# V made token-major for two head pairs in one product, in two half pairs of four

## The reference

```
xn  = layernorm(x)
K, Q, V = xn @ W_K[h], xn @ W_Q[h], xn @ W_V[h]        # per head h: 1024 x 64
attn = softmax(causal(Q K^T) / 8);  z = attn @ V;  a = concat(z) @ W_O^T
m = sum over the top 2 of 9 experts of w * (silu(xn Wg[e]) * (xn Wu[e])) @ Wd[e]
out = x + a + m
```

## Time and profile before

| | |
|---|---|
| median of 3 runs | 722.73 us |
| the profiled execution | 724.33 us, its span 722.4 us |
| granted TensorE clock, mean | 0.983 |
| busy: TensorE, VectorE, ScalarE, GpSimd | 97%, 87%, 78%, 67% |
| chain that ended last: TensorE, VectorE, DMA, GpSimd | 86%, 4%, 3%, 3% |
| one half of attention | 35.3 to 35.6 us |

### The profile page before, as it was taken

How to read it: one execution, slowest core, us unless ns; L and a number is a source line. 1 busy time by engine, 2 the same in 40 slices (tenths; PEclk the granted TensorE clock), 3 DMA queues, 4 the chain that set the end, 5 groups by cost and what they waited for, 6 DMA issues and landing times.

```text
span 722.4 us, 15068 instructions
## 1 busy us (share of the span) xinstructions
PE 698.1 (97%) x4877; PEld 607.4 (84%) x4877; DVE 629.8 (87%) x1401; ACT 564.5 (78%) x1312; POOL 487.2 (67%) x494
## 2 busy tenths in 40 slices
PE   7879999899999999999999999999999999999997
PEld 6659999778888888888888888888888888888886
DVE  8967777768999999999999999999999998998986
ACT  5915555568888888888888888888888888888873
POOL 5464444157677777878686878787878786868761
PEclk9869999989999999999999999999999999999999
DMA  8514722132434242424242424242515151515001
GB/s 237 165 30 111 168 75 58 44 90 69 92 74 105 54 103 63 107 52 107 59 107 52 106 62 111 49 116 50 125 34 130 36 135 24 136 27 139 19 2 59
DMA packets 50236, 61.05 MB, mean 85 GB/s; under 512 B 7440, under 2 KB 28272, under 8 KB 50160
## 3 DMA queue, kind: packets, MB, share of 16 engines
q1 hardware_dynamic: 47856, 55.36, 32.2%
q0 software_dynamic: 2304, 4.72, 2.6%
HBM read 12.87 MB, written 4.72 MB: 24 GB/s over the span
## 4 chain that ended last, share of the span: by engine, by line
PE 86%; DVE 4%; DMA 3%; POOL 3%; issue 2%; ACT 1%; SPq 0%; POOLq 0%
PE ps_big L1358 20%; PE ps_mid L1392 17%; PE ps_z L1413 7%; PE ps_z L1414 7%; PE ps_misc L1222 4%; PE ps_misc L1224 4%; PE ps_misc L1223 4%; PE ps_big L1413 3%; PE ps_big L1414 3%; PE ps_big L1311 3%; PE ps_big L1355 2%; DMA k_st<-k_st 2%; PE ps_z L1335 2%; PE ps_z L1336 2%; PE ps_misc L1240 2%
## 5 line engine op out<-in xcount | busy, mean ns | idle before, releaser
L669 POOL TENSOR_TENSOR probs<-probs,rden 128x1024 f32<-128x1024 f32 (+7 forms) x256 | 291.3, 1150 | 129.6 <-DVE rden L1118 128.6
L1083 DVE TENSOR_REDUCE neg_max<-ps_big 128x1 f32<-128x1024 f32 (+7 forms) x256 | 192.7, 753 | 31.0 <-PE ps_big L1358 27.4
L839 ACT ACTIVATE pT_hi<-ps_mid 128x512 fp32r<-128x512 f32 (+3 forms) x384 | 181.8, 491 | 45.9 <-PE ps_mid L1392 41.3
L1358 PE MATMUL ps_big<-k_st,q_st 128*128 128x512 f32 (+2 forms) x768 | 207.3, 379 | 3.5 <-ACT probs L826 3.0
L1129 DVE TENSOR_TENSOR pT_lo<-ps_mid,pT_hi 128x512 fp32r<-128x512 f32 (+3 forms) x384 | 204.0, 547 | 7.2 <-ACT pT_hi L839 6.4
L826 ACT ACTIVATE probs<-ps_big,neg_max 128x1024 f32<-128x1024 f32 (+7 forms) x256 | 190.2, 743 | 16.4 <-DVE neg_max L1083 13.8
L1392 PE MATMUL ps_mid<-ident,probs 128*128 128x128 f32 x1152 | 176.1, 275 | 3.2 <-DVE pT_lo L1129 1.9
L1392 PEld LDWEIGHTS ps_mid<-ident,probs 128*128 128x128 f32 x1152 | 138.0, 142 | 25.7 <-issue 7.8
L1358 PEld LDWEIGHTS ps_big<-k_st,q_st 128*128 128x128 f32 x768 | 119.2, 194 | 8.0 <-issue 2.2
L1413 PE MATMUL ps_z<-pT_hi,v_st 128*128 128x256 f32 x448 | 118.7, 297 | 0.0
L1414 PE MATMUL ps_z<-pT_lo,v_st 128*128 128x256 f32 x448 | 112.0, 282 | 0.0
(11 more groups left out here) (240 smaller groups left out, 1284.3 us busy)
## 6 DMA issues: line engine op xcount, KB each, us to landing
k_st<-k_st SPq DMA_DIRECT2D x90, 256.0 KB, 3.5
q_st<-q_parts SPq DMA_DIRECT2D x128, 128.0 KB, 3.1
y_dram<-y_sb SPq DMA_DIRECT2D x40, 64.0 KB
k_st<-k_parts SPq DMA_DIRECT2D x8, 256.0 KB
raw_gu<-in_L_ffn_Wg_dram SPq DMA_DIRECT2D x9, 176.0 KB, 2.9
raw_gu<-in_L_ffn_Wu_dram SPq DMA_DIRECT2D x9, 176.0 KB, 3.0
raw_d<-in_L_ffn_Wd_dram SPq DMA_DIRECT2D x9, 128.0 KB, 3.1
res<-in_L_attn_x_dram SPq DMA_DIRECT2D x4, 256.0 KB, 3.8
```

The costliest lines, as they stand in the source:

```text
L669: pool.tensor_tensor(rows, rows, col.to_broadcast([P, width]), ALU.mult).then_inc(normed, 1)
L839: nc.scalar.activation(pT_hi[:, t:t + 2 * tiles - 1:2, :], ps_mid[:, bank, 0:tiles * P].rearrange("p (t q) -> p t q", t=tiles), ACT.Copy). ...
L1083: nc.vector.tensor_reduce(neg_max[:, n:n + 1], ps_big[:, n % 2, off:off + width], AX_X, ALU.max, negate=True).then_inc(max_done, 1)
L1358: ins = nc.tensor.matmul(ps_big[:, n % 2, c0:c1], w, k_st[half][h][:, part, c0 - off:c1 - off], start=part == 0 and not masked, stop=part ...
```

## The change

The values are made token-major at once: a 128-token tile of `xT` is the stationary operand, and the weights of four heads (two head pairs, 256 columns) move. One step v0, v1, v2 or v3 makes two token tiles: two `product`s of three 128x256 matmuls. v2 and v3 stand where t0 and t1 stood; `vT` and the transpositions are gone. As the result serves pairs p and p+1, the four steps are made in halves 0, 3, 4, 7, 8, 11 and 12 only (`made`), "V halves" below, and in none of the others. Each of the four is copied by ScalarE and split by VectorE straight to `v_st`, now twice as large, and `ps_misc` is free after the split. `wqkv` transposes 4 weight tiles in one pair and 2 in the next, in place of 3. To make room, `probs1` and `probs3` are half as wide, and several tiles lie at other addresses; `raw_o` is loaded after the experts. Before the experts, four value steps stand in place of v0, v1, t0, t1; the last of them is copied and split amid the experts' weights.

```diff
-        PROJ_FIRST = ["wqkv", "q0", "q1", "k0", "k1", "v0", "v1", "t0", "t1"]
+        PROJ_FIRST = ["wqkv", "q0", "q1", "k0", "k1", "v0", "v1", "v2", "v3"]
...
         DVE_ORDER = read("""
...
-            L4.0 X9 R7 L4.1 Ck0 X10 R8 L5.0 L6.0 L6.1 X11 Co1- R9 R10 L7.0 X12 L8.0 Co0- L8.1 R11 R12 X13 L9.0
+            L4.0 X9 R7 L4.1 Ck0 X10 R8 L5.0 Cv0 L6.0 L6.1 X11 Co1- R9 R10 L7.0 X12 L8.0 Co0- L8.1 R11 R12 X13 L9.0
...
+        def made(a, name):
...
+            return 0 <= a < 2 * PAIRS - 1 and (name[0] != "v" or a % 4 in (0, 3))
...
+        def values_done(p, b):
+
+            a = 4 * (p // 2) - 1 + b
+            return proj_split, max(n + 1 for n, (at, name) in enumerate(SPLIT) if at == a and name[0] == "v")
...
         def bank_read(p, b, name):
...
-            return (proj_copied, proj_count(p, b, name)) if name[0] in "vk" else (proj_split, split_count(p, b, name))
+            return (proj_copied, proj_count(p, b, name)) if name[0] == "k" else (proj_split, split_count(p, b, name))
...
         @block.scalar
...
-                elif name[0] == "v":
-                    c = int(name[1])
-                    ins = nc.scalar.activation(vT[:, c * BLK:(c + 1) * BLK], bank, ACT.Copy)
                 else:
-                    c = int(name[1])
-                    ins = nc.scalar.activation(v_st[b_next][:, c * TPB:(c + 1) * TPB, :, 0, :],
-                                               bank.rearrange("p (t h c) -> p t h c", t=TPB, h=2), ACT.Copy)
+                    tiles = slice(2 * int(name[1]), 2 * int(name[1]) + 2)
+                    if p >= 0:
+                        wait(act, pv_done, 8 * (2 * p + b))
+                    ins = nc.scalar.activation(v_st[b_next][:, tiles, :, 0, :],
+                                               bank.rearrange("p (t h c) -> p t h c", t=2, h=4), ACT.Copy)
...
             for e in range(4, E):
                 split_expert(e)
+                if e == 6:
+                    act.wait_ge(tok_summed, 1)
+                    copy_proj(-1, 1, "v3", FIRST_BANK["v3"])
...
         @block.vector
...
-            for name in ("k1", "t0", "t1"):
+            for name in ("k1", "v0", "v1", "v2"):
                 split_proj(-1, 1, name, FIRST_BANK[name])
             dve.wait_ge(tok_summed, 1)
             nc.vector.tensor_copy(tok_i[:], ps_mid[:, 1, 0:SUBS]).then_inc(tok_ready, 1)
-            for e, part in DVE_LO[:8]:
+            for e, part in DVE_LO[:6]:
+                split_weights(e, part)
+            split_proj(-1, 1, "v3", FIRST_BANK["v3"])
+            for e, part in DVE_LO[6:8]:
                 split_weights(e, part)
...
         @block.tensor
...
-                    for t in range(TPB):
-                        kt = int(name[1]) * TPB + t
-                        ins = nc.tensor.transpose(bank[:, t * P:(t + 1) * P], vT[:, kt * P:(kt + 1) * P], ident[:])
+                    for t in range(2):
+                        tok = (half_next * QT + 2 * int(name[1]) + t) * P
+                        w = [part[:, 2:4, :].rearrange("p m r -> p (m r)") for part in (w_hi, w_lo)]
+                        ins = product(bank[:, t * 2 * P:(t + 1) * 2 * P], (xT_hi[:, tok:tok + P], xT_lo[:, tok:tok + P]), w)
```

More of the change, by code:

```diff
@@ L202, in bass_layernorm_causal_attention_plus_moe_kernel @@
         moe.close()
+        raw_o = sb("raw_o", [P, P])
+        part_raw = [sb(f"part_raw{j}", [P, BLK]) for j in range(2)]
         wo_hi = sb("wo_hi", [P, D], F32R)
@@ L209, in bass_layernorm_causal_attention_plus_moe_kernel @@
         v_st.append(v_stack(1))
-        probs = [sb(f"probs{j}", [P, S]) for j in range(4)]
+        probs = [sb(f"probs{j}", [P, BLK if j % 2 else S]) for j in range(4)]
         AREA = 2 * (QT + 2)
@@ L510, in stack @@
             def stack(p, b):
-                before, made = (p, 0) if b == 1 else (p - 1, 1)
-                for name in MISC_ORDER:
-                    if name[0] not in "qk":
-                        continue
-                    wait(sp, *part_done(before, made, name))
+                before, made_in = (p, 0) if b == 1 else (p - 1, 1)
+                names = [name for name in MISC_ORDER if name[0] in "qk"]
+                for n, name in enumerate(names):
+                    wait(sp, *part_done(before, made_in, name))
                     if name[0] == "k":
                         move_keys(p, b, name)
-                        if name != "k1":
-                            repeat_keys(p, b, name)
-                        continue
-                    for h in range(2):
-                        for half in range(2):
-                            stack_part(b, name, h, half)
-                    if name == "q0":
-                        repeat_keys(p, b, "k1")
+                    else:
+                        for h in range(2):
+                            for half in range(2):
+                                stack_part(b, name, h, half)
+                    if n and names[n - 1][0] == "k":
+                        repeat_keys(p, b, names[n - 1])
+                if names[-1][0] == "k":
+                    repeat_keys(p, b, names[-1])
             load_qkv(0)
@@ L530, in _ @@
                 load_expert(e)
-            load_o(0)
             for g in range(TB):
@@ L771, in _ @@
             split_expert(1, down=False)
-            for k in range(1, 9):
+            for k in range(1, 8):
                 if k == 5:
@@ L1224, in product, with fill_proj @@
                 return nc.tensor.matmul(dst, w[0], m[1], start=False, stop=stop, skip_group_check=True)
-            def fill_proj(name, half_next, bank=ps_misc[:, :]):
+            def fill_proj(name, half_next, bank=ps_misc[:, :], next_even=True):
                 if name == "wqkv":
-                    for m in range(3):
+                    for m in range(4 if next_even else 2):
                         ins = nc.tensor.transpose(bank[:, m * P:(m + 1) * P], raw_qkv[:, m, :], ident[:])
@@ L1404, in probs_v @@
                 if k0 == 0 and job == 0:
-                    before = p if b else p - 1
-                    pe.wait_ge(*part_done(before, 1 - b, last_of("t", before)))
+                    pe.wait_ge(*values_done(p, b))
                 tiles = 2 * m + 2
```

126 lines of the change are left out of this document (65 added, 61 removed).

## The result

The changed kernel took 730.76 us (median of 4 executions, 729.04 to 732.81) beside 722.47 (median of 4, 720.71 to 724.82) for the kernel before: ratio 1.0114, interval 1.0075 to 1.0153. Forecast were 725.3, "the same, slightly slower", and a range of 713 to 732: the time lies in the range, near its upper end, and "the same" by the prediction's own measure of 0.5% was wrong. It is slower, by 0.8 to 1.1%. One later execution of the kernel before took 1327.32 us, for a reason that was not found, and is left out of every ratio. The profiled executions are 729.04 against 724.33 us, spans 727.2 against 722.4.

What follows compares the result with a forecast made beforehand. TensorE was taken as busiest, with VectorE and the latencies of keys and one exp close behind. V halves +7.3, other halves -4.9, start +0.2 gave +2.6 us: 725.3 us as the median, range 713 to 732.

Steps and rivals of the forecast that it cites:

- The frame: Attention halves: two kinds, V halves about 36.5 us and others about 34.8, in the rhythm 0, 3, 4, 7, 8.
- TensorE's work: V halves: six 256-column matmuls per step at 0.12 us each, 0.56 us more work per V half.
- (E): Rival, V halves: loads of the new stationary operands show, 7 x 1.9 us more, 738.6 us; chance 0.03.
- Halves without values: Eight halves: of 2.28 us work removed, waits before S0 and S4 leave 4.9 us gained in all.
- The 0.36 forecast for v0 and v1: Before S0: keys' transfer leaves 0.36 us slack, so only that much of 1.40 us is kept, in seven halves.
- The forecast mark: Halves without values: TensorE stands about 1 us before S0, released by the keys' transfer.
- the term that was too small: V halves: TensorE work 3.9 us, waits at o1 2.0 and T14.0 1.4; together 7.3 us more.
- 7.3 - 4.9 + 0.2: Whole kernel: V halves' cost, less the other halves' gain, plus the start; +2.6 us.
- (A): Rival, whole kernel: TensorE's work is all that counts, 708.6 us; chance 0.09.
- (B): Rival, attention: VectorE and ScalarE run ahead, S4 does not wait, new splits hold nothing, 717.3 us; chance 0.18.
- (C): Rival, V halves: VectorE is the bound and its lag is handed on to every S, 730.3 us; chance 0.17.
- (D): Rival, start: late gate product keeps the granted clock low one expert step longer, some 2 us, 727.3 us; chance 0.07.

Runs made afterwards that it cites:

- e2: Changed kernel with values made only in half 0 and the start, later pairs reusing them (other output): 716.61 us, ratio 0.9885 to the kernel before.
- e1: Changed kernel with VectorE's value splits in halves 3, 4, 7, 8, 11, 12 narrowed to one column: 724.23 us, ratio 1.0003 to the kernel before.
- s2_before: Kernel before, cut to two head pairs in place of eight, to compare the start: 297.05 us.
- s2_after: Changed kernel, cut to two head pairs in place of eight, to compare the start: 296.19 us.
- e4: Changed kernel with two moves in TensorE's order alone, S15 before T11.0 and T0.0 before S4: 733.68 us, ratio 1.0125 to the kernel before.
- a2_after: Changed kernel, unaltered, run again in five more rounds beside the kernel before: 731.22 us, ratio 1.0081.

## Why the prediction was right and where it was wrong

**The frame held.** Halves in two kinds, in the rhythm forecast; less TensorE work and a longer kernel. The third key transfer is issued every 36.8 to 36.9 us around a V half of the changed kernel and every 34.5 to 35.5 else (forecast: 36.5 and 34.8).

**TensorE's work: right.** The six matmuls follow at 0.12 us. By the rule that the prediction took from the Trainium skill's page "TensorE: Matmul & The Clock Gate", section "The mechanism", each of these loads would be in the open; this is contradicted here as it was by the earlier trace rows. The prediction left out that the same section also lets a load run ahead where it goes to a background weight buffer, and the traces cannot tell which of the two sentences applies to these loads. Rival (E) had no part. Forecast were 0.56 us for a V half's work against the kernel before; e2 and e1 give 1.05 - 0.60 = 0.45.

**Halves without values: right in size, and in part by luck.** Forecast were 0.66 us kept per half, measured 0.60. S4 is as forecast: 0.29 kept (forecast 0.30), and the rest of the 0.88 of t0 and t1 is met by 0.38 of wait and 0.24 of restart. The 0.36 forecast for v0 and v1 came out at 0.02 by e2. The slack at the keys was read in the chain's times; S0's own start in the timeline lies some 0.17 before those (its mask matmul stands at 280.64 in the one and 280.81 in the other). The restart takes about 0.2, so that next to nothing of v1's 0.70 was kept. And of v0's 0.70, 0.14 to 0.16 was kept, since S11 waits for E9 and T6.1, which has `pT_split` among its waits, has a step of 0.33 and not 0.11; I had not looked for either. What makes up for both is the 0.28 between S4 and S9, forecast by nobody. The forecast mark was wrong too: TensorE does not stand 1 us before S0. It stands first at T11.0, whose L10.0 is queued behind X14's 1.23 us (0.41 and 0.19 of restart), and then at S0. I had looked for what holds S0, and not for what holds the transposition between v1's place and S0. That wait costs little by itself, but whoever shortens the keys' way meets it next.

**V halves: the term that was too small.** Forecast were 0.33 for o1, 0.2 for T14.0, nothing for v2 and v3, 0.53 together. By e1 it is 1.16, and in the one half that was laid side by side 0.54, 0.47 and 0.17. Places and releasers were right, `v_st` before o1 (2.1 us in the waits, 6 times, 0.36 each), `pT_lo` before T13.0 and T14.0. The price was that of the wait alone. The restart of 0.27 comes on top at o1 (0.63, of which e1 leaves 0.1), and 0.19 twice at T13.0/T14.0, since L12.0 and L12.1 end 0.6 later one by one and each holds its own transposition. That is shown by the steps of the chain, and that the splits are the cause by e1. The 0.17 of v2 and v3 show as a transposition that waits 0.07 and restarts at 292.98.

**The sum.** A V half costs 1.61 us more than before (forecast 1.09), a half without values 0.60 less: 2 x 1.61 - 2 x 0.60 = +2.02 us per turn. Over 14 stretches the first profile gives +4.1, in which the kernel before has one key transfer late by 0.8, and +0.7 up to the first o1 (half 0 and the start). The second profile of the changed kernel gives +5.3 and -1.0. The forecast had 7.3 - 4.9 + 0.2 = +2.6. The 5.9 us of the longer series agree with the profiles within their interval (4.8 and 4.3 against 4.0 to 7.8).

**The rivals.** (A) and (B) are out: the stretches of e2's turn are 34.4 to 35.5, not 33.3, and S4 waits. (C) has the time, 730.3, and half of the mechanism: VectorE's work does reach TensorE nearly whole (1.01 of its 1.2 us at the two new splits), but the lag is not handed on to every S. It is paid on the spot, in two named waits. Its own mark, a V half above 37 us, did not show (36.84 to 36.88; the one stretch of 37.17 in the second profile has a key transfer of 3.99 us). (D): the first gate product comes 0.95 us later in two executions whose granted clock is 1.00 up to 16 us (43.32 against 42.37), and the first score product after the experts stands at 136.00 in one execution of the changed kernel and 138.31 in the other, beside 137.94 before. s2_before and s2_after show no cost of it.

**The keys' transfer.** The page "DMA: Bandwidth & Descriptors" of the Trainium skill, section "Anatomy of one DMA", gave 2.6 us as an estimate, by a fit for transfers that GpSimd issues; SyncE issues these. Where such a transfer ends a wait in the changed kernel it takes 2.99 to 3.29, as the earlier trace rows had it.

## What to carry to other kernels

When an engine that is 97% busy is relieved, list for each removed piece everything that was being waited for under it, on all engines, and not only the consumer that you have in mind: here the keys' transfer and a VectorE split lay under the same product, and covering the one bought nothing (e4). An even load may count as well: the change gathered the value splits of two halves, two in each, into one, and by e1 the halves that have all four pay 1.16 us for them, while the others keep 0.60 of 2.28. No run spreads the steps evenly, so what that would give is open. And price a new wait on TensorE with its restart, here 0.19 to 0.27 us each, which can double a short one.

## What the runs showed of the hardware that was not expected

**The restart after a wait**, as above: a step of 0.23 us becomes 0.50 for a matmul of 512 columns, and 0.11 becomes 0.30 for a transposition. Of the 0.27 at o1, 0.16 is what a matmul of this size also has beyond its step when nothing waits (0.39 against 0.23). The other 0.11 is open. The trace has the weight load of o1 waiting with it (0.6 us at most, 6 times) and starting with it at 307.84, though `wo_hi`, which is o1's stationary operand and not `z_hi` as said ahead of the prediction, was there long before. That the load adds those 0.11 is argued and was not tested.

**The start has two lengths, some 3 us apart, in both kernels.** Two executions of the changed kernel (us, busy by engine, clock), the first profile and then a2_after:

```profile
12.00:16.00 4.00, 4.00 (x27) 4.00 (x27) 3.30 (x9) 1.99 (x4) 1.68 (x1) 0.66 0.89 274
```

```profile
12.00:16.00 4.00, 4.00 (x38) 4.00 (x38) 3.38 (x10) 3.13 (x8) 1.69 (x1) 1.00 0.71 212
```

The granted clock falls towards the lower level (0.50 is 1.2 GHz) within 12 to 16 us in the one and only later in the other (0.50 against 0.78 from 16 to 20 us), with TensorE busy without a break in those first 4 us in both, and the first gate product comes at 45.57 in place of 43.32. The cut-down kernel before shows it too (0.50 from 12 us on, gate product at 45.16). a2_after's ten times lie in two groups, 727.0 to 728.5 and 731.2 to 732.8. That these are the two starts is likely, but only one of the ten was profiled. What decides between them stays open. By my estimate from the two groups, half of their distance, a median of four executions is uncertain by 1.5 to 2 us, which is as much as some of the steps that are compared here.

**Late key transfers.** In e4 one third transfer (530.50 us) took 4.57 us in place of 3.03, and its stretch 39.39 in place of 36.2. In the kernel before one first transfer (592.05 us, ahead of the earlier trace rows) took 4.55 in place of 3.8. Others came in e2 (two first transfers, 4.54 and 4.57 us) and in the second profile of the changed kernel (4.54, and a third of 3.99). All of these end a wait of S0, since the keys have next to no slack. What made them late was not followed.
